# Laying minus the row maxima into the score banks from ScalarE and VectorE instead of adding them by a matmul, with a ring of three spare banks and VectorE taking 192 columns of the softmax sums

## The chip, the cores and the metric

The kernel runs on one core of a Trainium2 chip. The metric is the device time of one execution in microseconds (us), as the median over several executions. Before the change it is 2709.64 us (three runs, 2709.53 to 2709.69). Five engines take part: TensorE (PE; its weight loads are PEld), VectorE (DVE), ScalarE (ACT), GpSimd (POOL) and SyncE (SP), which issues the DMAs. Times inside the kernel are read from one profiled execution.

## The reference

A transformer layer in float32 on x of shape (2, 2048, 128), sandwich-normalised:

```python
x = x + layernorm(attention(layernorm(x)))      # 16 heads of 64, 2048 keys, full softmax
x = x + layernorm(ffn(layernorm(x)))            # low rank: 128 -> 32 -> 512 (gelu) -> 32 -> 128
# attention: q, k, v = x W + b ; attn = softmax(q k^T / 8) ; out = (attn v) Wo + bo
```

Nearly all of the work is attention: 2 batches x 16 heads x 2048 x 2048 scores, their exponentials, the sums of these and the product with v.

## The kernel before, in words

**Tiling.** Heads go in pairs (8 pairs), one pair and one batch make a *unit* (16), a unit has four *chunks* of 512 queries (64 chunks), and a chunk has 16 *steps* of 128 keys. All of the attention is 1024 steps. The main loop runs over 512 *doubles* n of two steps (2n and 2n+1); d = n % 8 is the place of a double in its chunk. Both heads of a pair are worked on in one instruction pair: the head's 64 dimensions fill one half of TensorE's rows, so the two matmuls of a pair run side by side.

**A step.** `scores(st)` writes a 128-key by 2x512-query tile into two PSUM banks (`score_ps[st % 2]`). It adds four matmul pairs: k_hi q_hi, k_hi q_lo, k_lo q_hi (float32 split into a high and a low float32r part) and a fourth, `one_row` times `m_rows`, which adds minus the row maximum of each query to every key. ScalarE then takes the exponential into `probs`, a ring of 8 steps (`act_exp`). `values(st)` multiplies it with v one double later. GpSimd adds the `probs` of a chunk up (`pool_add`, 1024 columns, 15 adds per chunk).

**The maxima** have to be known before a chunk's scores. `max_pair(n)` computes unsplit scores for 128 queries x 512 keys and both heads, and `dve_max` reduces them on VectorE (one instruction over 1024 columns). These run LEAD = 20 steps ahead. When a chunk's 16 are done, `dve_neg_max` and `transpose_max` (d = 6, `M_AT`) turn them, ScalarE copies them out, and `sp_m` lays them into `m_rows`.

**The order in a double** is written by hand: on TensorE first what is due at that d (K, V or Q projections, M, the output projection Wo), then `max_pair`, `scores(2n)`, `scores(2n+1)`, `max_pair`, `values(2n-2)`, `values(2n-1)`, and at d = 2 the denominators L. The other engines follow the same loop. Each engine runs its instructions strictly in the order written; semaphores tie them.

**Banks.** Of the eight PSUM banks four hold scores, two (`x0`, `x1`) the maxima's scores, one (`o`) the values' sum, and one (`misc`) K, Q, V, M, L, Wo and, from double 488 on, the feed-forward stages. `Pe.take` waits until the last user of a bank has been read.

**The end.** From double 488 on the feed-forward part of finished rows runs between the attention steps; ScalarE then changes tables between gelu and the exponential.

Of the kernel before, what the change touches and what calls it, by code (L numbers as in the profile page):

```python
# [39 lines left out]
K_AT = {(0, 0): 0, (0, 5): 1, (1, 0): 2, (1, 5): 3}  # L40
V_AT = {(2, 0): 0, (2, 5): 1, (3, 0): 2, (3, 5): 3}
L_AT, DENOM_OUT_AT, RECIP_AT, NEG_MAX_AT, NORM_AT = 2, 3, 5, 5, 7
Q_AT, M_AT = 4, 6
# [13 lines left out]

FREE_AT = (STEPS - LEAD) // 2
# [20 lines left out]
def ffn_banks():  # L79

    out, k = {}, 0
    for n in range(FFN_BASE[0], LAST):
        for half in range(2):
            for stage, g in ffn_pe(n, half):
                out[stage, g] = ["misc", "x0", "x1"][k % 3] if n > FREE_AT else "misc"
                k += 1
    return out


FFN_BANK = ffn_banks()  # L90


def build(nc, x, Wq, bq, Wk, bk, Wv, bv, Wo, bo, U1, V1, b1, U2, V2, b2, out):
# [11 lines left out]
    with ctx:  # L105
# [6 lines left out]
        one_row = sb("one_row", [P, P], F32R)  # L112
        m_rows = sb("m_rows", [P, M_RING, CH], F32R)
# [15 lines left out]
        denom = sb("denom", [P, 2, CH])  # L129
        denom_col = sb("denom_col", [P, CH // HD])  # L130
# [4 lines left out]
        max_rows = sb("max_rows", [2 * TC, 2, P], F32R)  # L135
# [26 lines left out]
        max_ps = psum("max_ps", [P, 2, CH])  # L162
        o_ps = psum("o_ps", [P, CH])
        misc_ps = psum("misc_ps", [P, CH])
        bank = {"s00": score_ps[0][:, 0, :], "s01": score_ps[0][:, 1, :], "s10": score_ps[1][:, 0, :],
                "s11": score_ps[1][:, 1, :], "x0": max_ps[:, 0, :], "x1": max_ps[:, 1, :],
                "o": o_ps[:], "misc": misc_ps[:]}
# [3 lines left out]
            m_evac m_dma0 m_dma1 m_dma2 score_ready exp_done pv_done sum_done denom_ps_ready  # L171
# [6 lines left out]
        m_dma = [s[f"m_dma{j}"] for j in range(M_RING)]  # L178
# [27 lines left out]
        def max_ps_of(n):  # L206
            return FIRST_MAX_PS[n % 3] if n < LEAD else max_ps


        class Pe:  # L210
# [4 lines left out]
            def take(self, name, kind, n):  # L215
# [19 lines left out]
                elif was == "scores":  # L235
                    pe.wait_ge(s["exp_done"], k + 1)
# [46 lines left out]
            def max_pair(self, n):  # L283
# [3 lines left out]
                if n < LEAD and n % 3:  # L287
                    self.take_pair((f"s{n % 3 - 1}0", f"s{n % 3 - 1}1"), "max", n)
                else:
                    self.take_pair(("x0", "x1"), "max", n)  # L290
# [4 lines left out]
                for h in range(2):  # L295
                    last = nc.tensor.matmul(max_ps_of(n)[:, h, :], q_hi[half(h), G % Q_RING, qt * P:(qt + 1) * P],  # L296
# [3 lines left out]
            def transpose_max(self, G):  # L300
                ps = self.take("misc", "M", G)
                self.pe.wait_ge(s["neg_max_done"], G + 1)
                nc.tensor.matmul(ps[0:HD, 0:P], neg_max[:, G % 2, :], ident[:], start=True, stop=True).then_inc(s["m_ps"], 1)

            def scores(self, st):
                pe = self.pe
                G, kt, u, b, j = st // T, st % T, st // (T * NC), st // (T * NC) % B, st % 2
                if kt == 0:
                    pe.wait_ge(s["q_split"], G + 1)
                    pe.wait_ge(m_dma[G % M_RING], 32 * (G // M_RING + 1))  # L310
                if st % (T * NC) == 0:
                    pe.wait_ge(s["k_split"], (u + 1) * NC)
                self.take_pair((f"s{j}0", f"s{j}1"), "scores", st)
                keys = slice(kt * P, (kt + 1) * P)
                for h in range(2):
                    nc.tensor.matmul(score_ps[j][:, h, :], k_hi[half(h), b, keys], q_hi[half(h), G % Q_RING, :],  # L316
                                     start=True, stop=False)
                for h in range(2):
                    nc.tensor.matmul(score_ps[j][:, h, :], k_hi[half(h), b, keys], q_lo[half(h), G % Q_RING, :],  # L319
                                     start=False, stop=False)  # L320
                for h in range(2):
                    nc.tensor.matmul(score_ps[j][:, h, :], k_lo[half(h), b, keys], q_hi[half(h), G % Q_RING, :],  # L322
                                     start=False, stop=False)
# [81 lines left out]
        def pe_program(pe):  # L405
# [43 lines left out]
            for n in range(DOUBLES, LAST):  # L449
# [4 lines left out]
                if n == END_L:  # L454
                    me.denominators(CHUNKS - 1)
# [5 lines left out]
        def act_k(act, u, c, name="misc"):  # L461
            n = u * NC + c
# [492 lines left out]
```

## Time and profile before

| what | us |
|---|---|
| median of the runs | 2709.64 |
| the profiled execution, its own time | 2711.64 |
| its span | 2709.8 |
| TensorE busy | 2619.6 (97%) |
| GpSimd busy | 2399.1 (89%) |
| VectorE busy | 1568.1 (58%) |
| ScalarE busy | 1250.3 (46%) |
| first exponential / last exponential start | 73.45 / 2653.72 |

The span is what the trace covers; the profiled execution took 1.8 us more than it. Busy time of TensorE counts overlapping matmuls once. A matmul's row shows its whole passage, so two neighbours overlap: the distance between their starts is what one costs. Start times are given from the start of the span.

### The profile page before, as it was taken

To read this page: it belongs to the slowest core of one execution; us is meant where nothing else is said; L and a number is where in the kernel's file an instruction comes from. 1 tells how busy PE (TensorE), PEld (TensorE's weight loads), DVE (VectorE), ACT (ScalarE), POOL (GpSimd) and SP (SyncE) were. 2 spreads that over 40 slices of the span, in tenths; PEclk is the share of its full clock that TensorE was granted. 3 is DMA by queue.
4 is the path that set the end of the run, shared out by engine and by line. 5 is a ranking of instruction groups with operands and counts; after the bars stand their busy time and mean duration, and the time that the engine had idled before them with its cause. 6 is when DMAs were issued, how large, how long until landed. Compare 5 with 4: busy or idle time off the path is not lost.

```text
span 2709.8 us, 44991 instructions
## 1 busy us (share of the span) xinstructions
PE 2619.6 (97%) x17520; PEld 1405.5 (52%) x17520; DVE 1568.1 (58%) x1827; ACT 1250.3 (46%) x1430; POOL 2399.1 (89%) x1099
## 2 busy tenths in 40 slices
PE   4999999999999999999999999999999999999886
PEld 2555555555555555555555555555555555554442
DVE  6555555555555555555555555555555555556756
ACT  2444444444444444444444444444444444443563
POOL 1899999999999999999999999999999999999673
PEclk7999999999999999999999999999999999999998
DMA  1000000000000000000000000000000000000000
GB/s 37 1 14 9 9 6 14 9 5 9 9 12 8 9 9 5 14 9 5 9 14 9 5 9 9 10 9 9 9 5 14 9 5 16 9 9 9 21 24 28
DMA packets 53309, 29.63 MB, mean 11 GB/s; under 512 B 26640, under 2 KB 44944, under 8 KB 53104
## 3 DMA queue, kind: packets, MB, share of 16 engines
q1 hardware_dynamic: 53104, 26.75, 3.6%
q8 instruction: 146, 2.39, 0.4%
q14 instruction: 59, 0.48, 0.1%
HBM read 23.85 MB, written 2.36 MB: 10 GB/s over the span
## 4 chain that ended last, share of the span: by engine, by line
PE 93%; DVE 5%; POOL 1%; issue 1%; DMA 0%; ACT 0%; POOLq 0%; DVEq 0%
PE o_ps L338 34%; PE max_ps L296 12%; PE score_ps L316 9%; PE score_ps L319 9%; PE score_ps L322 8%; PE score_ps L325 8%; PE misc_ps L270 2%; PE misc_ps L346 2%; PE misc_ps L355 2%; PE misc_ps L279 2%; PE misc_ps L261 2%; DVE max_part L616 1%; POOL total L776 1%; DVE ln_stats L574 1%; DVE y_acc L585 1%
## 5 line engine op out<-in xcount | busy, mean ns | idle before, releaser
L776 POOL TENSOR_TENSOR total<-total,probs 128x1024 f32<-128x1024 f32 x896 | 2131.8, 2379 | 193.7 <-ACT probs L491 85.3
L616 DVE TENSOR_REDUCE max_part<-max_ps 128x2 f32<-128x1024 f32 x1011 | 1238.0, 1225 | 888.0 <-PE max_ps L296 885.3
L491 ACT ACTIVATE probs<-score_ps 128x1024 f32<-128x1024 f32 x1024 | 997.9, 1025 | 823.4 <-PE score_ps L325 816.7
L338 PE MATMUL o_ps<-probs,v_sb 128*64 128x512 f32 x4096 | 1000.3, 609 | 0.0
L338 PEld LDWEIGHTS o_ps<-probs,v_sb 128*64 128x64 f32 x4096 | 249.5, 136 | 468.4 <-issue 315.8
L296 PE MATMUL max_ps<-k_hi,q_hi 64*128 64x512 f32 x2022 | 458.7, 448 | 14.1 <-DVE max_part L616 13.9
L316 PE MATMUL score_ps<-q_hi,k_hi 64*128 64x512 f32 x2048 | 408.4, 394 | 0.7 <-DVE max_part L616 0.7
L319 PE MATMUL score_ps<-q_lo,k_hi 64*128 64x512 f32 x2048 | 405.9, 391 | 0.0
L322 PE MATMUL score_ps<-q_hi,k_lo 64*128 64x512 f32 x2048 | 405.6, 391 | 0.0
L325 PE MATMUL score_ps<-m_rows,one_row 64*128 64x512 f32 x2048 | 403.1, 388 | 0.0
L296 PEld LDWEIGHTS max_ps<-k_hi,q_hi 64*128 64x128 f32 x2022 | 194.8, 185 | 338.9 <-issue 183.6
L322 PEld LDWEIGHTS score_ps<-q_hi,k_lo 64*128 64x128 f32 x2048 | 194.5, 185 | 44.4
L325 PEld LDWEIGHTS score_ps<-m_rows,one_row 64*128 64x128 f32 x2048 | 194.9, 185 | 43.3
L319 PEld LDWEIGHTS score_ps<-q_lo,k_hi 64*128 64x128 f32 x2048 | 194.9, 185 | 41.3
L316 PEld LDWEIGHTS score_ps<-q_hi,k_hi 64*128 64x128 f32 x2048 | 194.4, 186 | 26.0 <-issue 4.3
L776 POOL TENSOR_TENSOR total<-probs 128x1024 f32<-128x1024 f32 x64 | 152.8, 2388 | 17.6 <-ACT probs L491 17.6
L474 ACT ACTIVATE q_hi<-misc_ps,b_qk 128x512 fp32r<-128x512 f32 x64 | 44.1, 690 | 122.0 <-PE misc_ps L270 122.0
L654 DVE TENSOR_TENSOR y_acc<-misc_ps,y_acc 128x512 f32<-128x512 f32 x64 | 44.2, 691 | 92.8 <-PE misc_ps L355 92.8
L503 ACT ACTIVATE denom<-misc_ps 128x512 f32<-128x512 f32 x63 | 37.7, 598 | 128.9 <-PE misc_ps L346 128.9
L467 ACT ACTIVATE k_hi<-misc_ps,b_qk 128x512 fp32r<-128x512 f32 x60 | 41.3, 688 | 116.9 <-PE misc_ps L261 116.9
L608 DVE TENSOR_TENSOR v_sb<-misc_ps,b_v 128x512 f32<-128x512 f32 x60 | 41.5, 691 | 91.2 <-PE misc_ps L279 91.2
L780 POOL TENSOR_SCALAR ln_var<-ln_mv 128x4 f32<-128x4 f32 x32 | 8.1, 254 | 91.0 <-DVE ln_mv L578 91.0
(105 smaller groups left out, 1175.2 us busy)
## 6 DMA issues: line engine op xcount, KB each, us to landing
denom<-denom_scratch SPq DMA_DIRECT2D x126, 128.0 KB, 2.9
xg<-in_L_attn_x SPq DMA_DIRECT2D x14, 256.0 KB, 3.0
m_rows<-max_rows SPq DMA_DIRECT2D x128, 2.0 KB
block_out<-z_sb SPq DMA_DIRECT2D x8, 256.0 KB, 2.3
denom_col<-denom SPq DMA_DIRECT2D x126, 2.0 KB, 1.8
denom_scratch<-denom_col SPq DMA_DIRECT2D x63, 4.0 KB, 1.4
w_qkv<-in_L_attn_Wk SPq DMA_DIRECT2D x8, 64.0 KB, 1.9
w_qkv<-in_L_attn_Wq SPq DMA_DIRECT2D x8, 64.0 KB, 2.0
```

Source lines behind the costliest of these rows:

```text
L261: last = nc.tensor.matmul(ps[half(h), :], w_qkv[:, slot, 1, half(h)], xnT[:, cols], start=True, stop=True)
L270: last = nc.tensor.matmul(ps[half(h), :], w_qkv[:, slot, 0, half(h)], xnT[:, cols], start=True, stop=True)
L279: last = nc.tensor.matmul(ps[half(k), t * P:(t + 1) * P], xnT[:, at0:at0 + HD], w_qkv[:, slot, 2, :], start=True, stop=True)
L296: last = nc.tensor.matmul(max_ps_of(n)[:, h, :], q_hi[half(h), G % Q_RING, qt * P:(qt + 1) * P], k_hi[half(h), b, kc * CH:(kc + 1) * CH], ...
L316: nc.tensor.matmul(score_ps[j][:, h, :], k_hi[half(h), b, keys], q_hi[half(h), G % Q_RING, :], start=True, stop=False)
L319: nc.tensor.matmul(score_ps[j][:, h, :], k_hi[half(h), b, keys], q_lo[half(h), G % Q_RING, :], start=False, stop=False)
L322: nc.tensor.matmul(score_ps[j][:, h, :], k_lo[half(h), b, keys], q_hi[half(h), G % Q_RING, :], start=False, stop=False)
L325: last = nc.tensor.matmul(score_ps[j][:, h, :], one_row[half(h), :], m_rows[half(h), G % M_RING, :], start=False, stop=True)
L338: last = nc.tensor.matmul(o_ps[half(h), :], v_sb[:, b, kt, half(h)], probs[:, st % RING, h, :], start=(kt == 0), stop=(kt == T - 1))
L491: nc.scalar.activation(probs[:, st % RING], score_ps[st % 2][:], ACT.Exp, scale=SCALE).then_inc(s["exp_done"], 1)
L616: nc.vector.reduce_max(max_part[:, G % 2, :, qt, kc], max_ps_of(n)[:], AX.X).then_inc(s["max_done"], 1)
L776: nc.gpsimd.tensor_tensor(total[:, G % 2], so_far, probs[:, st % RING], ALU.add).then_inc(s["sum_done"], 1)
```

## The change

1. `scores` loses its fourth pair. The first three now *add* (`start=False`) to what lies in the bank: `act_seed` (ScalarE, even steps) and `dve_seed` (VectorE, odd steps) copy minus the maxima, held for all 128 partitions in `m_all`, into the two banks after the exponential of the step two before has read them. `scores(st)` waits for the seed instead of the exponential. Four matmuls ahead of the loop (`open_banks`) open the banks once.
2. `m_all` is filled through DRAM: `sp_m` writes 4 KB out, waits, and reads it back broadcast to 128 partitions (512 KB). It stands at d = 5 instead of 6; `neg_max` at d = 4 instead of 5.
3. The pair of maxima banks and `misc` become one ring of three, `r0` to `r2`; every user takes the next (`spare_banks`). `dve_max` becomes two instructions of 512 columns, one for each bank. LEAD is 22.
4. GpSimd adds 832 of the 1024 columns. VectorE sums the other 192 four steps at a time (`dve_part`, at even d) and merges the four results of a chunk (`dve_merge`, d = 1).
5. The denominators come as four 32-row products of 256 columns instead of two 64-row ones of 512, are copied out as 256 columns, and go to their column form in one DMA instead of two.
6. K and V projections of d = 5 move to d = 6.

The core of the diff:

```diff
-LEAD = 20
+SHARE, GROUP = 192, 4
+LEAD = 22
-K_AT = {(0, 0): 0, (0, 5): 1, (1, 0): 2, (1, 5): 3}
+K_AT = {(0, 0): 0, (0, 6): 1, (1, 0): 2, (1, 6): 3}
-L_AT, DENOM_OUT_AT, RECIP_AT, NEG_MAX_AT, NORM_AT = 2, 3, 5, 5, 7
-Q_AT, M_AT = 4, 6
+MERGE_AT, L_AT, DENOM_OUT_AT, RECIP_AT, NEG_MAX_AT, NORM_AT = 1, 2, 3, 5, 4, 7
+Q_AT, M_AT = 4, 5
...
             def scores(self, st):
...
-                self.take_pair((f"s{j}0", f"s{j}1"), "scores", st)
+                if j == 0:
+                    pe.wait_ge(s["seed_done"], st // 2 + 1)
+                else:
+                    pe.wait_ge(s["odd_seed_done"], st // 2 + 1)
...
-                for h in range(2):
-                    last = nc.tensor.matmul(score_ps[j][:, h, :], one_row[half(h), :], m_rows[half(h), G % M_RING, :],
-                                            start=False, stop=True)
...
+        def act_seed(act, st):
+            G = st // T
...
+                act.wait_ge(s["exp_done"], st - 1)
+            if st % T < 2:
+                act.wait_ge(m_dma[G % 2], 16 * (G // 2 + 1))
+            nc.scalar.activation(score_ps[0][:], m_all[:, G % 2], ACT.Copy).then_inc(s["seed_done"], 1)
+
+        def dve_seed(dve, st):
...
+            nc.vector.tensor_copy(score_ps[1][:], m_all[:, G % 2]).then_inc(s["odd_seed_done"], 1)
...
+        def dve_part(dve, k):
+            dve.wait_ge(s["exp_done"], (k + 1) * GROUP)
...
+            at = k * GROUP % RING
+            nc.vector.tensor_reduce(part_sum[:, k % (T // GROUP), :], probs[:, at:at + GROUP, 0, 0:SHARE].rearrange("p r n -> p n r"),
+                                    AX.X, ALU.add).then_inc(s["part_done"], 1)
+        def dve_merge(dve, G):
...
+            nc.vector.tensor_reduce(total[:, G % 2, 0, 0:SHARE], part_sum[:].rearrange("p g n -> p n g"),
+                                    AX.X, ALU.add).then_inc(s["merge_done"], 1)
...
                 act_exp(act, 2 * n)
                 act_exp(act, 2 * n + 1)
+                if n + 1 < DOUBLES:
+                    act_seed(act, 2 * n + 2)
...
+            sp.dma_start(m_dram[G % 2], max_rows[:, G % 2, :]).then_inc(s["m_out"], 16)
+            sp.wait_ge(s["m_out"], 16 * (G + 1))
+            sp.dma_start(m_all[:, G % 2].rearrange("p h n -> p (h n)"),
+                         m_dram[G % 2].rearrange("r n -> (r n)").partition_broadcast(P)).then_inc(m_dma[G % 2], 16)
```

On VectorE, in the middle of a chunk (doubles d = 1 to 5), stood before the output sum (`y_acc`), reductions of maxima, the low half of q, one of v, the reciprocal and the turned maxima:

```order
L654 TENSOR_TENSOR y_acc<-misc_ps,y_acc 128x512 [waits wo_ps_ready]
L616 TENSOR_REDUCE max_part<-max_ps 128x2 [waits max_ready] x7
L636 SCALAR_TENSOR_TENSOR q_lo<-misc_ps,b_qk,q_hi 128x512 [waits q_hi_done]
L616 TENSOR_REDUCE max_part<-max_ps 128x2 [waits max_ready]
L608 TENSOR_TENSOR v_sb<-misc_ps,b_v 128x512 [waits v_ps]
L616 TENSOR_REDUCE max_part<-max_ps 128x2 [waits max_ready]
L641 RECIPROCAL denom_col<-denom_col 128x8 [waits col_dma]
L616 TENSOR_REDUCE max_part<-max_ps 128x2 [waits max_ready]
L624 TENSOR_REDUCE neg_max<-max_part 128x8 [waits m_ps,max_done]
```

And from the same place on (d = 1 to the first half of d = 4) stands now:

```order
L740 TENSOR_TENSOR y_acc<-spare_ps,y_acc 128x512 [waits wo_ps_ready]
L684 TENSOR_REDUCE max_part<-spare_ps 128x1 [waits max_ready] x4
L545 COPY score_ps<-m_all 128x1024 [waits exp_done]
L722 TENSOR_REDUCE total<-part_sum 128x192 [waits denom_ps_ready,part_done]
L684 TENSOR_REDUCE max_part<-spare_ps 128x1 [waits max_ready] x4
L545 COPY score_ps<-m_all 128x1024 [waits exp_done]
L715 TENSOR_REDUCE part_sum<-probs 128x192 [waits merge_done,exp_done]
L684 TENSOR_REDUCE max_part<-spare_ps 128x1 [waits max_ready] x4
L545 COPY score_ps<-m_all 128x1024 [waits exp_done]
L684 TENSOR_REDUCE max_part<-spare_ps 128x1 [waits max_ready]
L706 SCALAR_TENSOR_TENSOR q_lo<-spare_ps,b_qk,q_hi 128x512 [waits q_hi_done]
L684 TENSOR_REDUCE max_part<-spare_ps 128x1 [waits max_ready] x3
```

Each double has four half-size reductions and one copy, every second double a partial sum, and the chunk one merge (of the L722 row).

On TensorE the scores of one double, and the maxima's matmuls behind them, stood before as:

```order
L316 MATMUL score_ps<-q_hi,k_hi 128x512 [waits exp_done]
L316 MATMUL score_ps<-q_hi,k_hi 128x512
L319 MATMUL score_ps<-q_lo,k_hi 128x512 x2
L322 MATMUL score_ps<-q_hi,k_lo 128x512 x2
L325 MATMUL score_ps<-m_rows,one_row 128x512 x2
L316 MATMUL score_ps<-q_hi,k_hi 128x512 [waits exp_done]
L316 MATMUL score_ps<-q_hi,k_hi 128x512
L319 MATMUL score_ps<-q_lo,k_hi 128x512 x2
L322 MATMUL score_ps<-q_hi,k_lo 128x512 x2
L325 MATMUL score_ps<-m_rows,one_row 128x512 x2
L296 MATMUL max_ps<-k_hi,q_hi 128x512 [waits max_done]
```

They stand now as:

```order
L345 MATMUL score_ps<-q_hi,k_hi 128x512 [waits seed_done]
L345 MATMUL score_ps<-q_hi,k_hi 128x512
L348 MATMUL score_ps<-q_lo,k_hi 128x512 x2
L351 MATMUL score_ps<-q_hi,k_lo 128x512 x2
L345 MATMUL score_ps<-q_hi,k_hi 128x512 [waits odd_seed_done]
L345 MATMUL score_ps<-q_hi,k_hi 128x512
L348 MATMUL score_ps<-q_lo,k_hi 128x512 x2
L351 MATMUL score_ps<-q_hi,k_lo 128x512 x2
L314 MATMUL spare_ps<-k_hi,q_hi 128x512 [waits max_done,m_evac]
```

The two pairs of L325 are gone, and the second pair of maxima (L314) now waits for the first pair of the same double to have been reduced, since the ring has only three banks.

## Rows read from the trace of the kernel before

**Rows 1.** Page, part 1: busy us (share of the span) x instructions.

```profile
PE 2619.6 (97%) x17520; PEld 1405.5 (52%) x17520; DVE 1568.1 (58%) x1827; ACT 1250.3 (46%) x1430; POOL 2399.1 (89%) x1099
```

**Rows 2.** Page, part 4: the chain that ended last, by engine.

```profile
PE 93%; DVE 5%; POOL 1%; issue 1%; DMA 0%; ACT 0%; POOLq 0%; DVEq 0%
```

**Rows 3.** Windows: stretch, its us, busy us of each engine, granted clock, DMA.

```profile
1200.00:1239.58 39.58, 39.58 (x260) 20.85 (x258) 22.48 (x24) 19.14 (x23) 36.79 (x17) 1.00 0.03 8
2480.00:2519.60 39.60, 33.12 (x198) 16.25 (x194) 29.97 (x50) 14.91 (x19) 31.93 (x17) 0.91 0.03 8
```

**Rows 4.** Timeline of VectorE: start us, us, instruction [idle before, releaser].

```profile
1198.84 1.23 DVE L616 TENSOR_REDUCE max_part<-max_ps 128x2 f32<-128x1024 f32 x1 [1.94 <-PE max_ps L296]
...
1204.08 1.23 DVE L616 TENSOR_REDUCE max_part<-max_ps 128x2 f32<-128x1024 f32 x1 [1.94 <-PE max_ps L296]
1205.22 0.74 DVE L631 SCALAR_TENSOR_TENSOR k_lo<-misc_ps,b_qk,k_hi 128x512 fp32r<-128x512 f32 x1
...
1208.68 1.23 DVE L616 TENSOR_REDUCE max_part<-max_ps 128x2 f32<-128x1024 f32 x1 [1.07 <-PE max_ps L296]
...
1213.07 1.23 DVE L616 TENSOR_REDUCE max_part<-max_ps 128x2 f32<-128x1024 f32 x1 [1.07 <-PE max_ps L296]
...
1238.42 1.23 DVE L616 TENSOR_REDUCE max_part<-max_ps 128x2 f32<-128x1024 f32 x1 [1.93 <-PE max_ps L296]
```

**Rows 5.** Timeline of all engines in one double.

```profile
1203.54 0.51 PE L296 MATMUL max_ps<-k_hi,q_hi 64*128 64x512 f32 x2
...
1203.88 0.40 PE L316 MATMUL score_ps<-q_hi,k_hi 64*128 64x512 f32 x2
...
1204.11 0.40 PE L319 MATMUL score_ps<-q_lo,k_hi 64*128 64x512 f32 x2
...
1205.01 1.95 ACT L491 ACTIVATE probs<-score_ps 128x1024 f32<-128x1024 f32 x2 [0.66 <-PE score_ps L325]
...
1205.71 0.42 PE L296 MATMUL max_ps<-k_hi,q_hi 64*128 64x512 f32 x2
...
1206.06 1.94 PE L338 MATMUL o_ps<-probs,v_sb 128*64 128x512 f32 x8
```

**Rows 6.** Timeline of TensorE: the denominators, and the four-tile product of the feed-forward part.

```profile
1231.68 1.03 PE L346 MATMUL misc_ps<-total,ones 128*64 128x512 f32 x4
1232.64 0.50 PE L296 MATMUL max_ps<-k_hi,q_hi 64*128 64x512 f32 x2
...
2540.71 1.07 PE L394 MATMUL misc_ps<-v_sb,u 128*32 128x512 f32 x8
```

**Rows 7.** Groups by line, 100 to 2500 us: busy us, mean ns | idle before.

```profile
L776 POOL TENSOR_TENSOR total<-total,probs 128x1024 f32<-128x1024 f32 x848 | 2016.3, 2378 | 165.2 <-ACT probs L491 60.9
L616 DVE TENSOR_REDUCE max_part<-max_ps 128x2 f32<-128x1024 f32 x969 | 1186.7, 1225 | 852.4 <-PE max_ps L296 849.6
...
L646 POOL TENSOR_TENSOR o_sb<-o_sb,denom 128x512 f32<-128x512 f32 x60 | 76.4, 1274 | 0.0
...
L654 DVE TENSOR_TENSOR y_acc<-misc_ps,y_acc 128x512 f32<-128x512 f32 x60 | 41.5, 692 | 90.0 <-PE misc_ps L355 90.0
```

**Rows 8.** Timeline of ScalarE: its one long copy out of SBUF.

```profile
26.49 3.50 ACT L544 ACTIVATE y_acc<-y_acc 128x3968 f32<-128x3968 f32 x1
```

**Rows 9.** Timeline of SP's queue; page, part 6: KB each, us to landing.

```profile
1207.52 1.10 SPq L860 DMA_DIRECT2D denom<-denom_scratch  x2
1208.72 1.30 SPq L848 DMA_DIRECT2D m_rows<-max_rows  x2
...
denom<-denom_scratch SPq DMA_DIRECT2D x126, 128.0 KB, 2.9
```

**Rows 10.** Line L585 of VectorE, 2480 to 2600 us: ns min/median/max.

```profile
L585 DVE TENSOR_SCALAR z_sb<-z_sb,ln_mv,ln_rstd x8: 314/340/2371, 2563.9 to 2592.4; 128x128 f32<-128x128 f32 x8
```

**Rows 11.** Timelines of VectorE and TensorE ahead of the loop, where the latter waits.

```profile
48.86 1.23 DVE L616 TENSOR_REDUCE max_part<-score_ps 128x2 f32<-128x1024 f32 x1 [2.00 <-PE score_ps L296]
...
50.23 0.80 PE L296 MATMUL score_ps<-k_hi,q_hi 64*128 64x512 f32 x2 [0.56 <-DVE max_part L616]
```

More of the change, by code:

```diff
@@ L76, in ffn_at, with spare_banks, use @@
     return [g for g in range(NG) if FFN_BASE[g] + offset == n]
[L79 to L86, printed above, removed]
+def spare_banks():
+    out = {}
+    def use(*key):
+        out[key] = f"r{len(out) % 3}"
+    for n in range(LAST):
+        G, u, c, d = n // PER_CHUNK, n // (PER_CHUNK * NC), n // PER_CHUNK % NC, n % PER_CHUNK
+        if n < DOUBLES:
+            if (c, d) in K_AT and u + 1 < UNITS:
+                use("K", (u + 1) * NC + K_AT[c, d])
+            if (c, d) in V_AT and u + 1 < UNITS:
+                use("V", (u + 1) * NC + V_AT[c, d])
+            if d == Q_AT and G + 2 < CHUNKS:
+                use("Q", G + 2)
+            if d == M_AT and G + 1 < CHUNKS:
+                use("M", G + 1)
+            if projected_at(G, d) is not None:
+                use("Wo", projected_at(G, d))
+        for stage, g in ffn_pe(n, 0):
+            use(stage, g)
+        if n < DOUBLES:
+            for st in (2 * n + LEAD, 2 * n + LEAD + 1):
+                for h in range(2 if st < STEPS else 0):
+                    use("max", 2 * st + h)
+        if n == END_L:
+            use("L", CHUNKS - 1)
+        if n == END_WO:
+            use("Wo", CHUNKS - 1)
+        for stage, g in ffn_pe(n, 1):
+            use(stage, g)
+        if n < DOUBLES and d == L_AT and G:
+            use("L", G - 1)
     return out
-FFN_BANK = ffn_banks()
+SPARE = spare_banks()
 def build(nc, x, Wq, bq, Wk, bk, Wv, bv, Wo, bo, U1, V1, b1, U2, V2, b2, out):
@@ L177, in build @@
         w_in = [s["w_in0"], s["w_in1"]]
-        m_dma = [s[f"m_dma{j}"] for j in range(M_RING)]
+        m_dma = [s["m_dma0"], s["m_dma1"]]
         W_DMA_N = 7 * 16
@@ L286, in max_pair @@
                 qt, kc = n % T // NC, n % NC
[L287 to L290, printed above, removed]
+                ps = [self.take(max_bank(n, h), "max", 2 * n + h) for h in range(2)]
                 if n % T == 0:
@@ L343, in denominators, with last_denominators @@
                 self.pe.wait_ge(s["sum_done"], (G + 1) * ADDS)
-                ps = self.take("misc", "L", G)
+                self.pe.wait_ge(s["merge_done"], G + 1)
+                ps = self.take(SPARE["L", G], "L", G)
+                for h in range(2):
+                    for k in range(2):
+                        at = (2 * h + k) * 32
+                        last = nc.tensor.matmul(ps[at:at + 32, 0:CH // 2], ones[:, 0:32],
+                                                total[:, G % 2, h, k * (CH // 2):(k + 1) * (CH // 2)], start=True, stop=True)
+                last.then_inc(s["denom_ps_ready"], 1)
+            def last_denominators(self, G):
+                self.pe.wait_ge(s["sum_done"], (G + 1) * ADDS)
+                self.pe.wait_ge(s["merge_done"], G + 1)
+                ps = self.take(SPARE["L", G], "L", G)
                 for h in range(2):
@@ L714, in dve_program @@
                 dve_v(dve, 0, c, FIRST_V_BANK[c])
[L715 removed]
+            dve_q(dve, 0, "r2")
             for n in range(LEAD):
[L717 removed]
+                for h in range(2):
+                    dve_max(dve, n, h)
                 if n == 5:
[L719 removed]
+                    dve_q(dve, 1, "r2")
                 if n + 2 in LATE_X_AFTER:
@@ L749, in dve_program @@
                 dve_low(dve, n)
+                if n == DOUBLES:
+                    dve_part(dve, STEPS // GROUP - 1)
+                    dve_merge(dve, CHUNKS - 1)
+                dve_z(dve, n)
                 if n == END_L:
```

228 lines of the change are left out of this document (126 added, 102 removed).

## The prediction

> **What bounds the kernel now.** I read the busy times first, then the chain, then windows of one chunk's length, then the timeline of single doubles. TensorE is busy 97% of the span [rows 1] and makes 93% of the chain [rows 2]. In the middle of the run it has no hole: 39.58 us busy in 39.58 us, at full granted clock, while VectorE works 22.48, ScalarE 19.14 and GpSimd 36.79 us [rows 3]. The same reduction of the same place in a chunk starts at 1198.84 and at 1238.42, so a chunk costs 39.58 us [rows 4]. Two plain doubles are 4.39 us apart (1208.68 to 1213.07). From about 72 us to about 2486 us this is 61 chunks of one length; the three last, with the feed-forward part between them, have TensorE busy only 33.12 of 39.60 us at a clock of 0.91 [rows 3] and are another regime.
>
> So the question is not only how much TensorE saves, but which engine is next. GpSimd is at 93% of a chunk, and VectorE's idle 17 us are what the change spends.
>
> **TensorE's side.** Score pairs start 0.23 us apart (1203.88, 1204.11) [rows 5]. The change takes away one pair per step, 16 per chunk: 16 x 0.228 = 3.65 us. The denominators take 0.96 us to the next start, of which 0.11 is the restart that the row behind them always pays, so 0.86 [rows 6]. In the new form each instruction has half the columns and four 32-column tiles have to run side by side. They do: the four-tile product of the feed-forward part has 8 instructions of 512 columns in 1.07 us, as long as the denominators' 4 [rows 6]. So L costs 0.43 and saves 0.43. TensorE alone would need 39.58 - 3.65 - 0.43 = 35.5 us per chunk, a plain double 3.93.
>
> **VectorE's side, per chunk.** A reduction of 1024 columns takes 1225 ns, an operation on 512 columns 692 ns [rows 7]: 1.04 ns per column and 0.16 us fixed. Neighbours overlap: k_lo starts 1.14 us after a reduction that lasts 1.23 (1204.08, 1205.22) [rows 4]. So 1024 columns occupy 1.13 us, 512 0.60, and 768 0.86.
> - Maxima: 32 x 0.60 = 19.2 (16 x 1.13 = 18.1 before).
> - Odd seeds: 8 copies of 1024 columns. The trace has no copy into PSUM on VectorE. Bounds: 0.60 if it ran at two columns per cycle, 1.23 if nothing overlapped. I take the reduction's 1.13, the nearest row of equal size: 9.1.
> - Partial sums and merge: 5 reductions of 768 elements, 4.3. They read four elements 4 KB apart (merge: 768 B apart) for each result, and no row of VectorE reads so. Lower bound 0.86 each, upper bound twice the per-column time, 1.66.
> - One q, one y, two of k or v: 2 x 0.65 + 2 x 0.60 = 2.5; reciprocal and neg_max 0.3.
>
> Sum 35.4 us: as much as TensorE's 35.5. Two engines of equal load can't both be full unless each may run ahead of the other, and here they hardly may: the ring has three banks, so the second pair of maxima in a double needs the first half of the first pair reduced (and k or q read, where one stands between). I therefore work out a chunk double by double.
>
> Within a double, from TensorE's start: the first maxima are ready at 0.54 (1203.54 to 1204.08) [rows 4, 5], the first scores start at 0.34, the second pair of maxima at 0.34 + 6 x 0.23 = 1.72 and is ready 0.46 later, the values end the double 2.21 after that pair. Work due at the start (K, V, Q, Wo) adds 0.85, M 0.21. From the end of what VectorE owes to TensorE's next start I count 0.20 (0.09 of overlap, 0.14 from the end of the row at 50.09 to 50.23, less a little for the full clock) [rows 11], and 0.10 for TensorE's restart. VectorE works in order: first half, second half, both halves of the second pair, seed (when the exponential of step 2n+1 is done, at 3.19), at even d the partial sum.
> - After an even double VectorE comes free 1.4 to 1.6 us into the next one; its first half ends at about 2.0 and the second pair starts at 2.2 instead of 1.72. Doubles d = 5 and 7 become 0.61 and 0.58 late.
> - d = 1 starts as late and has y first: 0.38. d = 2 follows the merge: 0.53.
> - d = 4 has q between the halves, which ends at 2.65 + 0.20 = 2.85 instead of 2.57: 0.38. K at d = 0 and 6 likewise 0.38 each, V 0, since it is read first.
> - d = 3 follows a double that the denominators lengthen: 0.
>
> Sum 3.24 us in chunks with K, 2.48 with V, mean 2.86. A chunk is 35.5 + 2.86 = 38.34 us, that is 1.24 less than before; over 61 chunks -76 us.
>
> **What lies beside.** The even seed on ScalarE: 1024 columns, from 3.50 us for 3968 [rows 8] 0.83 ns per column and 0.2 fixed, 1.05 us. The two exponentials take 1.95 [rows 5] and start at 1.24, so the seed is done at about 4.15 and is needed at 3.93 + 0.34 = 4.27 in the tightest (plain) double: hidden, by 0.1 us. ScalarE's chunk is 19.1 + 8 x 0.95 = 26.7 of 38: not a bound. If that 0.1 is gone, d = 3 pays it, 6 us in all. GpSimd: 2378 ns for 1024 columns and 1274 for 512 [rows 7] are 2.16 ns per column, so 832 columns take 1.96; 15 x 1.96 + 1.27 = 30.7 us instead of 36.8: it leaves the field. The maxima's way through DRAM: SP must first see the reciprocal (3.1 us into d = 5), the denominators' DMAs [rows 9] follow 1.4 later and take 1.1 to issue; the 4 KB go out at 5.7 and land by about 8 at the latest, and the 512 KB are estimated from the 128 KB that land in 2.9 us [rows 9] at 3.5 to 4.5: there at 11.5 to 12.5. The first seeds of the next chunk stand 12.8 us after d = 5 begins. Hidden, with 0.3 to 1.3 us left; each us beyond would cost 61.
>
> **Start and end.** The first seed needs the DMA chain (about 5.5 us behind the turned maxima instead of 2), and two more maxima pairs stand ahead: first exponential some 3 us later, of which two pairs saved at the end give 1 back: +2. In the last three chunks VectorE gets some 45 us more of work in a stretch of 224, in series with the normalisations, while TensorE has 11 us less and GpSimd is shorter: +5, between -15 and +30.
>
> Sum: 2709.8 - 76 + 2 + 5 = 2641 us of span. The profiled execution took 1.8 us more than its span, the median of the runs 0.2 less than it; against the median the forecast is 2641 us.
>
> **A rule on ports.** VectorE's normalisations, SBUF to SBUF, take 314 ns alone and up to 2371 beside GpSimd's additions [rows 10]: they wait for each other. Would the seed, too, which reads SBUF and writes PSUM? The Trainium skill (SBUF — State Buffer, "Who interferes with whom") says that only copies in a two-port mode share GpSimd's port, and that this mode needs source and destination in SBUF; by it the seed neither waits nor runs at double speed, and the sum stands. No run shows this form yet.
>
> **A rule that speaks against the change.** The partial sums jump 4 KB from element to element. The Trainium skill (Advanced Engine Details and Errata, "SBUF Cachelines") says that every access in a new 16-byte line pays a penalty, without a figure. No row here shows a strided read; by that rule the third rival below would hold.
>
> **The rivals.**
> - *TensorE keeps the bound.* If a seed costs 0.6 us, VectorE has 31.2 us per chunk, is free at 0.9 to 1.0 after an even double and delays only the k and q doubles: 36 to 36.5 us per chunk, 2709.8 - 61 x 3.3 = about 2510; with no delay at all 2709.8 - 61 x 4.08 = 2461. For it: TensorE has no hole today. Against: no row shows such a copy, and the ring is tight. Chance 0.13.
> - *Hand-overs eat the gain.* Each of seven late doubles pays 0.18 us more than I count (two semaphores for a bank, the DMA way late): 39.58 again. About 2700 to 2740. Chance 0.15.
> - *The strided sums cost more: slower.* Place: `dve_part`, `dve_merge`. VectorE bears its load without idling, so what they cost more goes into the chunk nearly whole. It decides from 1.24 / 5 = 0.25 us per reduction on; at 1.66 us (0.80 more) a chunk is 38.3 + 4.0 = 42.3, the run 2709.8 + 61 x 2.8 = about 2880; at half of that 2760. Chance 0.15.
> - *The seed waits for GpSimd's additions.* Eight waits of about 1 us per chunk: 46 us per chunk, near 3120. Against: VectorE's reductions beside the same additions hold at 1225 ns [rows 7]; but they don't read SBUF. Chance 0.04.
>
> **How the numbers follow.** Forecast 0.53 (own range 2590 to 2700), rivals 0.13, 0.15, 0.15, 0.04. The range 2505 to 2775 leaves out the lower half of the first rival (0.06), the upper part of the third (0.09) and the fourth (0.04). A measurement of this kernel tells 0.2% (5.4 us) from no change. Faster: 0.53 less 0.02, 0.13 and a third of the second, together 0.70; same 0.05; slower 0.25.
>
> **What the profile after would show.** In a chunk TensorE busy about 35.5 of 38.3 us with its idle time in front of the second pair of maxima, released by VectorE's reductions; VectorE busy 37 to 39 us by its rows (overlaps counted once); seed rows of 1.2 us on VectorE and 1.05 on ScalarE; reductions of 512 columns 0.69; partial sums 0.96; additions 1.96; no idle time put down to DMAs of m_all. The prediction is wrong if partial sums exceed 1.2 us, if seeds are near 0.7 or over 2 us, or if a chunk in the middle is under 37 or over 39.6 us.

## The result, and the profile after

The changed kernel takes 2840.77 us (median of four runs, 2840.3 to 2841.39), the kernel before 2709.59 beside it: a ratio of 1.0484 (95% interval 1.0466 to 1.0503), slower by 4.8%. The forecast of 2641 us is wrong in sign, and the range ended at 2775.

Parts 1, 4 and 5 of the page of the changed kernel, over its whole span; the form of the lines is that of [rows 1, 2, 7]:

```profile
PE 2484.4 (88%) x15728; PEld 1206.7 (43%) x15728; DVE 2627.9 (93%) x3683; ACT 1702.0 (60%) x1942; POOL 2003.7 (71%) x1095
...
DVE 57%; PE 36%; issue 6%; ACT 1%; DMA 0%; POOL 0%; POOLq 0%; DVEq 0%; ACTq 0%
...
L885 POOL TENSOR_TENSOR total<-total,probs 128x832 f32<-128x832 f32 x896 | 1762.8, 1967 | 592.1 <-ACT probs L555 527.6
L684 DVE TENSOR_REDUCE max_part<-spare_ps 128x1 f32<-128x512 f32 x2020 | 1307.8, 684 | 135.1 <-PE spare_ps L314 110.8
...
L545 DVE COPY score_ps<-m_all 128x1024 f32<-128x1024 f32 x512 | 623.5, 1218 | 16.7 <-ACT probs L555 16.5
L534 ACT ACTIVATE score_ps<-m_all 128x1024 f32<-128x1024 f32 x512 | 530.0, 1035 | 9.4 <-PE score_ps L328 6.2
...
L715 DVE TENSOR_REDUCE part_sum<-probs 128x192 f32<-128x768 f32 x256 | 392.1, 1531 | 1.8 <-ACT probs L555 1.8
...
L722 DVE TENSOR_REDUCE total<-part_sum 128x192 f32<-128x768 f32 x64 | 97.9, 1530 | 0.0
```

VectorE went from 58 to 93% and from 5 to 57% of the chain. Every new row is where it was put, except the last two: a partial sum of 768 elements takes 1531 ns, where a reduction of 1024 took 1225 before [rows 7].

A window of 41 us, a little under one chunk (41.55, below), in the form of [rows 3]; then VectorE over parts of three of its doubles (d = 1 to 3), as in [rows 4]:

```profile
1200.00:1241.00 41.00, 36.89 (x242) 17.88 (x238) 38.63 (x52) 25.50 (x29) 30.44 (x16) 1.00 0.07 20
```

```profile
1201.31 2.66 DVE L684 TENSOR_REDUCE max_part<-spare_ps 128x1 f32<-128x512 f32 x4
1203.89 1.22 DVE L545 COPY score_ps<-m_all 128x1024 f32<-128x1024 f32 x1
1205.02 1.53 DVE L722 TENSOR_REDUCE total<-part_sum 128x192 f32<-128x768 f32 x1
1206.46 2.66 DVE L684 TENSOR_REDUCE max_part<-spare_ps 128x1 f32<-128x512 f32 x4
1209.04 1.22 DVE L545 COPY score_ps<-m_all 128x1024 f32<-128x1024 f32 x1
1210.16 1.52 DVE L715 TENSOR_REDUCE part_sum<-probs 128x192 f32<-128x768 f32 x1
```

The starts give what each occupies, that is, the time to the next start: the copy 1.13 us (1203.89 to 1205.02), as forecast; the merge 1.44 (to 1206.46), where 0.86 was taken. VectorE never rests in this stretch, and TensorE waits for it at the second pair of maxima:

```profile
1205.94 0.39 PE L351 MATMUL score_ps<-q_hi,k_lo 64*128 64x512 f32 x2
1207.29 0.50 PE L314 MATMUL spare_ps<-k_hi,q_hi 64*128 64x512 f32 x2 [0.96 <-DVE max_part L684]
```

Waits of the changed kernel from 100 to 2500 us (who waited for whom: us in total, times, longest):

```profile
POOL total L885 <- ACT probs L555: 570.1, 405, 2.9
...
PEld spare_ps L314 <- DVE max_part L684: 254.7, 234, 1.4
PE spare_ps L314 <- DVE max_part L684: 216.5, 275, 1.0
...
DVE max_part L684 <- PE spare_ps L314: 92.3, 158, 0.7
...
ACT score_ps L534 <- DMA m_all<-m_scratch: 1.6, 4, 0.6
```

VectorE waited 849.6 us for TensorE's maxima before [rows 7] and 92.3 now; TensorE's matmuls of the maxima waited 6.4 us for VectorE before and 216.5 now. The wait has changed sides. The way through DRAM is hidden: 1.6 us in all.

From the copies of the denominators, one per chunk, comes the length of a chunk (line L503 before, L567 after; first and last start):

Before:

```profile
L503 ACT ACTIVATE denom<-misc_ps x58: 598/598/599, 124.4 to 2380.4; 128x512 f32<-128x512 f32 x58
```

After:

```profile
L567 ACT ACTIVATE denom<-spare_ps x55: 384/385/388, 130.3 to 2373.8; 128x256 f32<-128x256 f32 x55
```

(2380.4 - 124.4) / 57 = 39.58 us before, (2373.8 - 130.3) / 54 = 41.55 after. 61 chunks x 1.97 = 120 of the 129 us by which the spans differ; start and end have the other 9.

### The profile page after: what moved, and what is told of

Read it like the earlier page. It is cut to its first block, busy times and chain, and to the rows that moved or that the text cites. A ratio compares the mean times of both kernels' runs of the same rounds, so it can differ in the third digit from the quotient of the medians.

```text
span 2838.7 us, 44015 instructions
## 1 busy us (share of the span) xinstructions
PE 2484.4 (88%) x15728; PEld 1206.7 (43%) x15728; DVE 2627.9 (93%) x3683; ACT 1702.0 (60%) x1942; POOL 2003.7 (71%) x1095
## 4 chain that ended last, share of the span: by engine, by line
DVE 57%; PE 36%; issue 6%; ACT 1%; DMA 0%; POOL 0%; POOLq 0%; DVEq 0%; ACTq 0%
DVE max_part L684 22%; PE o_ps L364 14%; DVE score_ps L545 12%; DVE part_sum L715 12%; PE spare_ps L314 10%; DVE total L722 3%; PE spare_ps L282 2%; PE spare_ps L291 2%; PE spare_ps L300 2%; PE score_ps L345 2%; DVE q_lo L706 1%; PE score_ps L351 1%; PE score_ps L348 1%; DVE k_lo L700 1%; DVE y_acc L740 1%
## 5 line engine op out<-in xcount | busy, mean ns | idle before, releaser
L885 POOL TENSOR_TENSOR total<-total,probs 128x832 f32<-128x832 f32 x896 | 1762.8, 1967 | 592.1 <-ACT probs L555 527.6
L684 DVE TENSOR_REDUCE max_part<-spare_ps 128x1 f32<-128x512 f32 x2020 | 1307.8, 684 | 135.1 <-PE spare_ps L314 110.8
L314 PE MATMUL spare_ps<-k_hi,q_hi 64*128 64x512 f32 x2020 | 500.5, 487 | 268.0 <-DVE max_part L684 241.1
L545 DVE COPY score_ps<-m_all 128x1024 f32<-128x1024 f32 x512 | 623.5, 1218 | 16.7 <-ACT probs L555 16.5
L534 ACT ACTIVATE score_ps<-m_all 128x1024 f32<-128x1024 f32 x512 | 530.0, 1035 | 9.4 <-PE score_ps L328 6.2
L314 PEld LDWEIGHTS spare_ps<-k_hi,q_hi 64*128 64x128 f32 x2020 | 200.2, 184 | 715.7 <-issue 305.0
L715 DVE TENSOR_REDUCE part_sum<-probs 128x192 f32<-128x768 f32 x256 | 392.1, 1531 | 1.8 <-ACT probs L555 1.8
L885 POOL TENSOR_TENSOR total<-probs 128x832 f32<-128x832 f32 x64 | 125.7, 1965 | 130.0 <-ACT probs L555 130.0
L516 ACT ACTIVATE q_hi<-spare_ps,b_qk 128x512 fp32r<-128x512 f32 x64 | 44.1, 690 | 91.7 <-PE spare_ps L291 91.7
L722 DVE TENSOR_REDUCE total<-part_sum 128x192 f32<-128x768 f32 x64 | 97.9, 1530 | 0.0
L567 ACT ACTIVATE denom<-spare_ps 128x256 f32<-128x256 f32 x63 | 24.3, 385 | 110.3 <-PE spare_ps L376 110.3
```

The lines of the kernel that those rows point to most:

```text
L314: last = nc.tensor.matmul(ps[h], q_hi[half(h), G % Q_RING, qt * P:(qt + 1) * P], k_hi[half(h), b, kc * CH:(kc + 1) * CH], start=True, stop ...
L534: nc.scalar.activation(score_ps[0][:], m_all[:, G % 2], ACT.Copy).then_inc(s["seed_done"], 1)
L545: nc.vector.tensor_copy(score_ps[1][:], m_all[:, G % 2]).then_inc(s["odd_seed_done"], 1)
L684: nc.vector.reduce_max(max_part[:, G % 2, h, qt, kc:kc + 1], bank[max_bank(n, h)], AX.X).then_inc(s["max_done"], 1)
L715: nc.vector.tensor_reduce(part_sum[:, k % (T // GROUP), :], probs[:, at:at + GROUP, 0, 0:SHARE].rearrange("p r n -> p n r"), AX.X, ALU.add ...
L722: nc.vector.tensor_reduce(total[:, G % 2, 0, 0:SHARE], part_sum[:].rearrange("p g n -> p n g"), AX.X, ALU.add).then_inc(s["merge_done"], 1)
```

## The experiments

The theory after the result: the strided reductions (those that step over a distance in SBUF from one element to the next) cost 0.58 us more apiece than forecast, and since VectorE sets the pace, five of them per chunk make 2.9 us. Rivals: the seeds, a further hand-over on the way of the scores; the ring of three banks; additions on GpSimd. Chunk lengths below come from the denominators' copies, as above; each ratio is to the kernel before, run beside that version (medians 2704.8 to 2706.35 us).

**The price of a strided read by itself (p1).** The kernel before, with a loop over the forms at the end of VectorE's program; its core is this, and a similar loop makes the additions. It ran once, and only its trace is used:

```diff
+            for v in forms:
+                nc.vector.tensor_reduce(res[:, 0:v.shape[1]], v, AX.X, ALU.add).then_inc(s["probe"], 1)
```

> The kernel before, with extra reductions and additions on VectorE behind its last work, one at a time: 768 elements in rows of four whose neighbours are 4 B, 8 B, 16 B, 32 B, 192 B (168 elements there) and 4 KB apart, 768 B apart, then rows of two and of eight with neighbours 4 KB apart, and additions of 768 elements with the first input's neighbours 4, 8 and 32 B apart. Theory (the distance inside SBUF is what costs): 0.96 us for neighbours 4 B apart, 1.53 us for 4 KB and for every distance over some line size, with rows of two and eight at the same 1.53. Rival (the short rows are what costs, not the distance): 1.53 us for all rows of four, less for rows of eight (about 1.25), more for rows of two (about 2.1).

VectorE's timeline behind its last work (the rows of four at 4, 8, 16, 32 B, 4 KB and 768 B, the rows of two and of eight at 4 KB; then additions with neighbours 4 and 32 B apart; the shorter form at 192 B is left out):

```profile
2705.41 0.95 DVE L781 TENSOR_REDUCE o_sb<-probs 128x192 f32<-128x768 f32 x1
...
2706.40 0.95 DVE L781 TENSOR_REDUCE o_sb<-probs 128x192 f32<-128x768 f32 x1
...
2707.39 1.50 DVE L781 TENSOR_REDUCE o_sb<-probs 128x192 f32<-128x768 f32 x1
...
2708.92 1.52 DVE L781 TENSOR_REDUCE o_sb<-probs 128x192 f32<-128x768 f32 x1
...
2710.95 1.45 DVE L781 TENSOR_REDUCE o_sb<-probs 128x192 f32<-128x768 f32 x1
...
2712.43 1.45 DVE L781 TENSOR_REDUCE o_sb<-probs 128x192 f32<-128x768 f32 x1
...
2713.92 0.96 DVE L781 TENSOR_REDUCE o_sb<-probs 128x384 f32<-128x768 f32 x1
...
2714.92 1.47 DVE L781 TENSOR_REDUCE o_sb<-probs 128x96 f32<-128x768 f32 x1
...
2716.42 0.96 DVE L785 TENSOR_TENSOR o_sb<-probs 128x768 f32<-128x768 f32 x1
...
2718.41 1.53 DVE L785 TENSOR_TENSOR o_sb<-probs 128x768 f32<-128x768 f32 x1
```

Not the short rows cost but the distance: 0.95 us with neighbours up to 8 B apart, 1.45 to 1.52 from 16 B on; additions go from 0.96 at 4 B to 1.53 at 32 B. The rows of two at 4 KB, however, cost nothing more (0.96), which the theory had at 1.53. The Trainium skill (Advanced Engine Details and Errata, "SBUF Cachelines") has full speed where a 16-byte line is hit at least twice, and a penalty where each access goes to another line; the step between 8 and 16 B agrees. In the rows of two each access goes to another line than the one before it, without a penalty; there the measurement decides. In the changed kernel the same read takes 1531 ns, 0.08 us more than here; what makes that up is not shown.

**As many sums, from neighbouring elements (e1).** The output is then wrong: the right elements are left out of the sums. The merge is changed in the same way.

```diff
-probs[:, at:at + GROUP, 0, 0:SHARE].rearrange("p r n -> p n r")
+probs[:, at].rearrange("p h n -> p (h n)")[:, 0:SHARE * GROUP].rearrange("p (n r) -> p n r", r=GROUP)
```

> The changed kernel, but the partial sums and the merge read 768 neighbouring elements in rows of four, so they add the wrong elements; same count, same places. Theory (the strided read makes the partial sums 1.53 us instead of 0.96, and this decides): they take 0.96 us, a chunk goes from 41.5 to about 38.7 us (5 x 0.57 less), the run to about 2840 - 61 x 2.8 = 2670 us, faster than before. Rival (the chunk is held by the hand-overs between VectorE and TensorE, and the sums fill idle time): over 2780 us.

Measured 2657.2 us, ratio 0.9817 (0.9802 to 0.9831). By line, 100 to 2300 us, and the denominators:

```profile
L715 DVE TENSOR_REDUCE part_sum<-probs 128x192 f32<-128x768 f32 x229 | 216.0, 943 | 0.0
```

```profile
L567 ACT ACTIVATE denom<-spare_ps x59: 384/385/388, 128.2 to 2366.8; 128x256 f32<-128x256 f32 x59
```

A chunk is 38.60 us. The distance between elements alone is worth 2.95 us per chunk and turns the sign: 5 x 0.58 = 2.9.

TensorE's pairs of maxima in two doubles of this version, the first two lines in d = 2 and the others in d = 3:

```profile
1203.70 0.50 PE L314 MATMUL spare_ps<-k_hi,q_hi 64*128 64x512 f32 x2
1205.96 0.50 PE L314 MATMUL spare_ps<-k_hi,q_hi 64*128 64x512 f32 x2 [0.38 <-DVE max_part L684]
1208.83 0.50 PE L314 MATMUL spare_ps<-k_hi,q_hi 64*128 64x512 f32 x2
1210.54 0.47 PE L314 MATMUL spare_ps<-k_hi,q_hi 64*128 64x512 f32 x2
```

The second pair starts 2.26 us after the first in d = 2 and 1.71 in d = 3, which is not held up: 0.55 late, where the forecast has 0.43 (its 0.53 counts 0.10 for the restart). The seven doubles that follow d = 2 come out within 0.07 us of the forecast's list.

**The sums left out (e3).** `dve_part` and `dve_merge` are not issued, so 192 columns are missing from the sums.

> The changed kernel without partial sums and merge on VectorE; GpSimd still adds 832 columns, so 192 of the 1024 columns are summed by nobody (the output is wrong by that). Theory (VectorE's load sets the chunk until TensorE's 35.5 us is reached; only the k, q and late doubles then wait): a chunk of 36 to 36.7 us, 2840 - 61 x 5.2 = about 2520 us. Rival (seeds and ring hold the chunk by themselves): above 38 us per chunk, over 2620 us.

Measured 2509.29 us, ratio 0.9277 (0.9262 to 0.9293), a chunk of 36.68 us. With seeds and ring as they are, the chunk is within 1.2 us of the 35.5 forecast for TensorE alone. The rival falls.

**GpSimd adds everything (e2).** `others(tile)` takes all 1024 columns, the sums on VectorE go.

> The changed kernel with SHARE = 0: GpSimd adds all 1024 columns again, VectorE sums nothing. GpSimd then has 15 x 2.38 + 1.27 = 37.0 us per chunk. Theory: GpSimd becomes the bound, a chunk of 37.0 to 37.6 us, about 2840 - 61 x 4.2 = 2585 us, clearly faster than the kernel before. Rival (the seeds and the three-bank ring, not the sums, made it slower): over 2700 us.

Measured 2684.32 us, ratio 0.9913 (0.9894 to 0.9933), a chunk of 38.68 us: a little below the kernel before, under the rival's 2700, but 100 us above the theory. GpSimd's timeline:

```profile
1204.86 30.13 POOL L875 TENSOR_TENSOR total<-total,probs 128x1024 f32<-128x1024 f32 x12
1234.94 1.28 POOL L729 TENSOR_TENSOR o_sb<-o_sb,denom 128x512 f32<-128x512 f32 x1
1236.17 4.91 POOL L875 TENSOR_TENSOR total<-total,probs 128x1024 f32<-128x1024 f32 x2
```

Twelve additions of 2.38 us take 30.13: each starts 2.51 us after the last, as it waits for it. So GpSimd needs about 15 x 2.51 + 1.27 = 38.9 us per chunk, and TensorE waits for it, at the output projection (100 to 2300 us):

```profile
PE spare_ps L392 <- POOL o_sb L729: 96.1, 56, 2.6
```

Its busy time of 36.79 [rows 3] hid that it, too, stood within 1 us of the chunk before the change: without some relief there, the saved matmuls could bring about 1 us per chunk and no more.

**One part alone: the strided sums in the kernel before (e9).** `dve_part`, `dve_merge` and GpSimd's 832 columns, no seeds, banks as before.

> The kernel before with one part of the change alone: VectorE sums 192 columns by the strided reductions (and merges), GpSimd adds 832. VectorE gets 7.2 us more per chunk and has 17 us idle. Theory (a strided reduction costs time only where VectorE is full): within 0.5% of the kernel before, a chunk of 39.6 us. Rival (the strided reads disturb others, or the reductions delay the maxima and so TensorE by themselves): 1% slower and more; the second pair of maxima then waits for VectorE.

Measured 2728.83 us, ratio 1.0078 (1.0063 to 1.0093), a chunk of 39.77 us. That is between the two and fits neither: 7.2 us more of work on VectorE cost 0.2 us per chunk where it has 17 idle. VectorE's timeline suggests where:

```profile
1217.22 1.52 DVE L649 TENSOR_REDUCE part_sum<-probs 128x192 f32<-128x768 f32 x1
1218.67 1.21 DVE L620 TENSOR_REDUCE max_part<-max_ps 128x2 f32<-128x1024 f32 x1
```

The next maxima, at 1218.67, begin the moment the sum is done; elsewhere they wait for TensorE. That such delays are what TensorE pays for is argued, not shown. 61 chunks x 0.19 = 12 us are half of the 22 us by which this version is longer than the kernel before beside it (2706.35); the rest I have not placed.

**The seeds (e6).** The odd seeds go to ScalarE, the strided sums stay.

```diff
                     act_seed(act, 2 * n + 2)
+                    act_odd_seed(act, 2 * n + 3)
...
-                if n + 1 < DOUBLES:
-                    dve_seed(dve, 2 * n + 3)
```

> The changed kernel with the odd seeds on ScalarE too, behind the even ones; the strided sums stay. VectorE loses 8 x 1.13 = 9 us per chunk, ScalarE has 26.7 + 8 x 0.95 = 34.3. Theory (VectorE's load is what made the change slower): a chunk of 36 to 37.5 us, 2510 to 2600 us. Rival (seeding itself, a hand-over more between the exponential and the scores, is the cost): the odd scores then wait for two exponentials and two copies, 3.9 us in a row, a chunk over 39.5 us, over 2720 us.

Measured 2534.74 us, ratio 0.9371 (0.9357 to 0.9385), a chunk of 37.18 us. Page, parts 1 and 4:

```profile
PE 2432.0 (96%) x15728; PEld 1193.8 (47%) x15728; DVE 2068.0 (82%) x3171; ACT 2162.4 (85%) x2454; POOL 2008.2 (79%) x1095
...
PE 84%; DVE 12%; issue 1%; ACT 1%; DMA 1%; POOL 0%; SPq 0%; POOLq 0%; ACTq 0%; DVEq 0%
```

The same seeds and the same slow sums, and TensorE makes the chain again. Seeding is not the cost; VectorE's load is. Both the time and the chunk are as the theory has them.

**The banks (e7).** r0 and r1 for the maxima only, r2 for the rest.

```diff
-        out[key] = f"r{len(out) % 3}"
+        out[key] = f"r{key[1] % 2}" if key[0] == "max" else "r2"
```

> The changed kernel with the banks used as before the change: r0 and r1 for the two halves of the maxima, r2 for all else; the rest as it is. Theory (VectorE works without a pause only while TensorE's second pair of maxima comes early enough; with a pair of banks it must wait for both halves, and VectorE then idles some 0.6 us per double): a chunk of 45 to 46 us, 3050 to 3130 us. Rival (VectorE's work alone sets the time, the banks don't matter): within 20 us of the changed kernel's 2840.

Measured 3178.82 us, ratio 1.175 (1.1733 to 1.1768), a chunk of 46.37 us: the theory's mechanism, but more than it expected at most (46 us, and 3130 for the run). Its waits, 100 to 2300 us:

```profile
PEld spare_ps L314 <- DVE max_part L684: 639.3, 475, 2.0
...
DVE max_part L684 <- PE spare_ps L314: 323.8, 475, 0.7
```

Each waits for the other 475 times. The ring of three is worth 4.8 us per chunk to the changed kernel.

**A smaller share (e8).** `SHARE = 64`.

> The changed kernel with SHARE = 64: strided reductions of 256 elements (0.16 + 256 x 1.79 ns = 0.62 us) instead of 768, GpSimd adds 960 columns at 2.24 + 0.13 us each (its additions start 0.13 us after the end of the one before): 36.8 us per chunk. Theory (VectorE and GpSimd both near 37): a chunk of 37 to 38 us, 2570 to 2640 us, less than with SHARE = 0 (2684) and 192 (2840). Rival (any share on VectorE costs more than it frees on GpSimd): over 2684 us.

Measured 2578.75 us, ratio 0.9533 (0.9518 to 0.9547), a chunk of 37.28 us, as the theory has it. Shares 0, 64 and 192 give 38.68, 37.28 and 41.55 us: GpSimd's chain on the one side, VectorE's strided sums on the other.

**The sums by additions (e5).**

```diff
+            nc.vector.tensor_tensor(tmp if q else acc, probs[:, at:at + 2, 0, 0:SHARE], probs[:, at + 2:at + 4, 0, 0:SHARE],
+                                    ALU.add).then_inc(s["part_done"], 1)
+            if q:
+                dve.wait_ge(s["part_done"], k + 1)
+                nc.vector.tensor_tensor(acc, acc, tmp, ALU.add).then_inc(s["acc_done"], 1)
```

> The changed kernel with the 192 columns summed by tensor_tensor additions of neighbouring elements (per four steps one of 2 x 192 and one more into the running sum, one of 192 per chunk) instead of strided reductions; the output is the reference's. Own work about 4 x 0.46 + 3 x 0.46 + 0.26 = 3.5 us per chunk instead of 5 x 1.44 = 7.2. Theory (only VectorE's time counts): a chunk of about 38 us, some 2635 us, faster than before. Rival (an addition with both inputs in SBUF waits for GpSimd's additions, as the normalisations do): 8 waits of about 1 us, a mean row of 1.3 us and more instead of 0.55, a chunk of 42 us or more, over 2800 us.

Measured 3366.1 us, ratio 1.2445 (1.2424 to 1.2466), a chunk of 49.86 us. By line, 100 to 2300 us:

```profile
L718 DVE TENSOR_TENSOR part_sum<-probs 128x384 f32<-128x384 f32 x177 | 286.1, 1616 | 0.0
L722 DVE TENSOR_TENSOR part_sum<-part_sum 128x384 f32<-128x384 f32 x133 | 194.3, 1461 | 4.6
...
L728 DVE TENSOR_TENSOR total<-part_sum 128x192 f32<-128x192 f32 x44 | 50.1, 1140 | 0.0
```

The rival holds, by far more than its 2800 us; the theory does not. The rows of 384 elements take 1.5 to 1.6 us on average beside GpSimd, while 768 took 0.96 in p1, where GpSimd had stopped. The same run has one that falls into a pause of GpSimd, and takes 0.56 us (GpSimd's addition ends at 1224.23, the next starts at 1226.14):

```profile
1222.26 1.97 POOL L891 TENSOR_TENSOR total<-probs 128x832 f32<-128x832 f32 x1 [4.72 <-ACT probs L555]
1224.68 0.56 DVE L722 TENSOR_TENSOR part_sum<-part_sum 128x384 f32<-128x384 f32 x1
```

So the additions wait for GpSimd's, as the normalisations do [rows 10]. The Trainium skill (SBUF — State Buffer, "Who interferes with whom") says that a VectorE instruction with two SBUF inputs contends with a GpSimd instruction that reads SBUF, and one with a single SBUF input outside the two-port modes does not; the prediction had told only the part on copies. The trace agrees on the first. On the second it agrees for the seeds, which take 1218 ns in every run that has them on VectorE, and for e1's reductions of neighbouring elements (943 ns beside GpSimd, 0.95 us in p1 without it); the strided reductions of 768, 1514 to 1543 ns on average by run, stay 0.06 to 0.09 us above p1's.

These rows account for 4 x 1.616 + 3 x 1.461 + 1.140 = 12.0 us of VectorE per chunk where the strided sums took 7.7, which is 4.3 of the 8.3 us more. Most of the rest lies in TensorE's clock. Where two such additions follow each other, the maxima come late and TensorE stands still for about 3 us or more; what follows runs slowly:

```profile
1214.40 0.80 PE L314 MATMUL spare_ps<-k_hi,q_hi 64*128 64x512 f32 x2 [3.32 <-DVE max_part L684]
1215.13 3.07 PE L364 MATMUL o_ps<-probs,v_sb 128*64 128x512 f32 x8
```

The granted clock was 1.00 from 1207 to 1211 us and 0.51 from 1214 to 1217: the lower of the two levels, 1.2 GHz instead of 2.4. Between 100 and 2300 us the eight matmuls of the values are seen whole 343 times; 86 times, each after such a pause, they take 3.35 us on average, all other times 1.94 at most; in the changed kernel, where TensorE never waits over 1.02 us in that stretch, they always take 1.94. An estimate from these rows is 86 x (1.41 + 0.19) / 44 = 3.1 us per chunk, the 0.19 for the slow pair ahead. That it enters the time whole is argued. TensorE's mean granted clock was 0.902 in this run and 0.979 in the changed kernel.

**The fast version with a smaller share (e10).** e6 with `SHARE = 128`.

> All seeds on ScalarE as in the fast version, and SHARE = 128: strided reductions of 512 elements (0.16 + 0.92 = 1.08 us instead of 1.53), GpSimd adds 896 columns, 15 x (2.10 + 0.13) + 1.27 = 34.7 us per chunk. Theory (TensorE is the bound there and both helpers stay below 35.5): within 15 us of that version's 2535, rather lower since VectorE's late doubles get shorter. Rival (GpSimd's chain of additions is near enough to decide): over 2550 us.

Measured 2525.54 us, ratio 0.9333 (0.9317 to 0.9348), a chunk of 37.03 us. That is within 15 us of e6 and lower, as the theory has it. No other version that computes the whole reference was as fast here: it is 6.7% below the kernel before, 11% below the changed one.

## Why the prediction was wrong

**The step that failed** is the one term "Partial sums and merge: 5 reductions of 768 elements, 4.3", at 0.86 us each. They occupy 1.44, 7.2 us per chunk. Both bounds were given (0.86 and 1.66), it was said that no row showed such a read, and the lower end went into the sum without a reason. The trace held no evidence for either end, so the choice was not one that it could carry; the rule on cache lines stood beside it, and the rival that rests on it was given a chance of 0.15. The kernel behaves as that third rival said: with the measured price its way of reckoning gives 38.34 + 5 x 0.58 = 41.2 us, and 41.55 were measured. The range ended at 2775 us, which left out the upper part of that rival, where the result lies. e1, p1 and e3 together show the cause: the same instructions in the same places without the distance give the forecast's chunk.

**What held, by its own steps.**
- TensorE: pairs 0.23 us apart; the four denominators' tiles side by side, 0.57 us to the next start against 0.96 before, so 0.39 saved of 0.43 forecast.
- The double-by-double sum of the late doubles, 38.34 us per chunk, was for sums at 0.86 us. e1 is that kernel: 38.60. Its run, 2657, is 16 us from the forecast of 2641, and inside the forecast's own range. The coupling through the three banks was right in mechanism and size, as the pairs of maxima in e1 show; e7 bears out the mechanism (46.37 us per chunk, against 45 to 46 expected). The sum itself is 38.36 if redone from its rounded terms.
- Seeds: 1.22 us on VectorE and 1.04 on ScalarE against 1.23 and 1.05; none at double speed, none waiting for GpSimd. The even seed is hidden: TensorE waited 3.4 us for it in the whole run.
- m_all: 3.7 us to landing within 3.5 to 4.5, hidden.
- Start and end: +9 against +7.

**What was right by luck.** That GpSimd would leave the field came true on a wrong sum. It was put at 30.7 us per chunk from its busy rows. Its additions start 0.13 us later than their rows end, so it is 15 x 2.097 + 1.27 = 32.7, and 38.9 with 1024 columns. With 832 columns nothing hangs on it, but the 93% of a chunk before were too low: it was at 98%.

**The rivals.** "TensorE keeps the bound" was argued from a faster seed, which did not come; e3 and e6 reach that regime by taking load off VectorE. "Hand-overs eat the gain" asked for 1.24 us per chunk beyond the count and falls with e1, which has 0.26. "The seed waits for GpSimd" falls with the seed's 1218 ns.

## What to carry to other kernels

When two engines come out with equal loads, the sum of each is not the time: work out who waits for whom in one period, bank by bank, and then ask how much one more unit of work on either costs. Here it was nearly its whole price. A term with two bounds, of which one turns the sign of the forecast, decides the forecast; it deserves the nearest thing to a measurement, or a range that reaches to both. And an engine that waits for its own last instruction is busier than its busy time says: read the distance of starts.

## What the runs showed of the hardware

- In reductions VectorE read four-byte elements from SBUF at about 1.04 ns each with neighbours 4 or 8 B apart, and at about 1.75 ns from 16 B on (0.95 and 1.50 us for 768 in p1). An addition whose first input had neighbours 32 B apart took 1.53 us, with 4 B 0.96. Rows of two elements 4 KB apart, with the next row's beside them, were free (0.96 us); rows of four and eight were not (1.45, 1.47). In the kernels, 4 KB apart, 256, 512 and 768 elements took 606, 1073 and 1531 ns (e8, e10, the changed kernel).
- A VectorE addition with both inputs in SBUF took 1.6 us on average for 384 elements beside GpSimd's additions, up to 2.35, and 0.56 in a pause of GpSimd in the same run (e5). GpSimd's additions grew from 1967 to 1991 ns on average, its normalisation of 512 columns from 1275 to 1580.
- GpSimd's additions that wait for the one before start 0.13 us after its end (e2: rows of 2.38 us, starts 2.51 apart).
- After TensorE had stood still for 3.3 us, the granted clock was 0.51 over the next 3 us, and the values' eight matmuls took 3.07 us instead of 1.94 (e5).
- Values that ScalarE or VectorE wrote into a PSUM bank were added to by matmuls with `start=False`, once one matmul with `start=True` had written the bank (the changed kernel, e2 and e5 to e8).
